# Attention block: the row maxima reach their contiguous row tile by tile, and the first score buffer gets its maximum behind its scores

## The reference

```python
x = x + attn(layernorm(x))      # softmax(q @ k.T * 64**-0.5) @ v for 16 heads, @ w_out + b_out
x = x + ffn(layernorm(x))       # fp4_linear(silu(fp4_linear(x, w_gate)) * fp4_linear(x, w_up), w_down)
```

## Time and profile before

| | us |
|---|---|
| median of 3 runs | 1384.71 |
| lowest, highest | 1379.86, 1384.8 |
| the profiled execution | 1384.4 |
| its span, first to last instruction | 1381.5 |
| TensorE busy | 1299.0 |
| GpSimd busy | 1053.9 |
| ScalarE busy | 897.7 |
| VectorE busy | 798.2 |

### The profile page before, as it was taken

How to read it: one execution, slowest core, us unless ns; L and a number is a source line. 1 busy time by engine, 2 the same in 40 slices (tenths; PEclk the granted TensorE clock), 3 DMA queues, 4 the chain that set the end, 5 groups by cost and what they waited for, 6 DMA issues and landing times.

```text
span 1381.5 us, 24376 instructions
## 1 busy us (share of the span) xinstructions
PE 1299.0 (94%) x7541; PEld 674.4 (49%) x7541; DVE 798.2 (58%) x2142; ACT 897.7 (65%) x1300; POOL 1053.9 (76%) x457
## 2 busy tenths in 40 slices
PE   4999999999999999999999999999999999898466
PEld 3555555555455555555445555555555454343245
DVE  6655555555455555555555555555555556777694
ACT  4767666677666766677666676667767667554242
POOL 4488878898778878888788888888988888789232
PEclk9999999999999999999999999999999999999787
DMA  2000000000000000000000000000000000000001
GB/s 61 2 9 2 1 2 9 2 1 1 3 9 2 2 1 9 2 1 1 3 9 2 2 1 9 2 2 1 3 1 1 1 2 1 2 1 1 1 1 30
DMA packets 18300, 6.63 MB, mean 5 GB/s; under 512 B 9696, under 2 KB 18016, under 8 KB 18160
## 3 DMA queue, kind: packets, MB, share of 16 engines
q1 hardware_dynamic: 17936, 4.40, 1.4%
q0 software_dynamic: 224, 0.54, 0.1%
HBM read 3.75 MB, written 1.05 MB: 3 GB/s over the span
## 4 chain that ended last, share of the span: by engine, by line
PE 85%; DVE 7%; issue 4%; POOL 2%; ACT 0%; DMA 0%; POOLq 0%; SPq 0%; DVEq 0%; ACTq 0%
PE o_ps L1151 32%; PE s_ps L1000 24%; PE mx_ps L1023 7%; PE mx_ps L1016 5%; PE misc_ps L1141 3%; PE s_ps L1008 2%; PE misc_ps L1133 2%; PE misc_ps L971 2%; PE misc_ps L983 1%; PE misc_ps L972 1%; PE misc_ps L973 1%; POOL acc_pool L497 1%; PE misc_ps L984 1%; PE misc_ps L985 1%; PE s_ps L1243 1%
## 5 line engine op out<-in xcount | busy, mean ns | idle before, releaser
L497 POOL TENSOR_TENSOR acc_pool<-acc_pool,probs 128x1024 f32<-128x1024 f32 x352 | 853.4, 2424 | 49.5 <-POOL acc_pool L497 40.3
L614 ACT ACTIVATE probs<-s_ps 128x1024 f32<-128x1024 f32 x512 | 527.3, 1030 | 122.1 <-PE s_ps L1008 67.3
L790 DVE CUSTOM_DVE_ANT_0 summed<-mx_ps,rise 128x512 bf16<-128x512 f32 x503 | 344.8, 686 | 424.9 <-issue 354.5
L1151 PE MATMUL o_ps<-probs,vv 128*64 128x512 f32 x2048 | 498.5, 607 | 5.1 <-ACT probs L614 5.1
L534 ACT ACTIVATE rise<-mx_ps 128x512 f32<-128x512 f32 x503 | 301.2, 599 | 271.7 <-PE mx_ps L1016 261.1
L1151 PEld LDWEIGHTS o_ps<-probs,vv 128*64 128x64 f32 x2048 | 127.2, 136 | 229.5 <-issue 174.8
L1016 PE MATMUL mx_ps<-k_raw,q_hi 64*128 64x512 f32 x503 | 224.5, 446 | 10.5 <-DVE part_max L790 9.2
L1023 PE MATMUL mx_ps<-k_hi,q_hi 64*128 64x512 f32 x503 | 224.5, 446 | 1.9 <-DVE part_max L790 1.8
L1000 PE MATMUL s_ps<-q_hi,k_hi 64*128 64x512 f32 x1024 | 207.0, 399 | 0.9 <-ACT probs L614 0.8
L1000 PE MATMUL s_ps<-q_hi,k_lo 64*128 64x512 f32 x1024 | 202.6, 390 | 0.0
L1000 PE MATMUL s_ps<-q_lo,k_hi 64*128 64x512 f32 x1024 | 202.4, 390 | 0.0
(11 more groups left out here) (161 smaller groups left out, 1119.0 us busy)
## 6 DMA issues: line engine op xcount, KB each, us to landing
wqkv<-in_L_attn_w_qkv SPq DMA_DIRECT2D x8, 192.0 KB, 3.3
y<-in_L_attn_x SPq DMA_DIRECT2D x4, 256.0 KB, 4.6
mrow<-neg_max SPq DMA_DIRECT2D x64, 2.0 KB, 2.0
out<-y SPq DMA_DIRECT2D x4, 256.0 KB, 2.3
wo<-in_L_attn_w_out SPq DMA_DIRECT2D x8, 64.0 KB, 1.9
wx<-in_L_ffn_w_down POOLq DMA_DIRECT2D x1, 176.0 KB, 6.6
wx<-in_L_ffn_w_gate POOLq DMA_DIRECT2D x1, 128.0 KB, 4.3
wx<-in_L_ffn_w_up POOLq DMA_DIRECT2D x1, 128.0 KB, 4.9
```

The lines of the kernel that those rows point to most:

```text
L497: pool.tensor_tensor(acc, first, probs[:, j % P_BUFS, :, :], ALU.add) \
L614: act.activation(probs[:, j % P_BUFS, :, :], s_ps[:, j % 2, :, :], ACT.Exp, scale=SCALE) \
L790: dve.tensor_tensor_reduce(summed[:, s % 2, :], mx_bank(h, pair), rise[:, h, :], 1.0, LOWEST, ALU.add, ALU.max, part_max[:, slot:slot + 1] ...
L1151: ins = pe.matmul(o_ps[DH * h:DH * (h + 1), :], vv[par(w)][:, j, DH * h:DH * (h + 1)], probs[:, j % P_BUFS, h, :], start=(j == 0), stop=(j ...
```

## The change

The reduction is made four times, once for each query tile `t`, as soon as that tile's last column is there (at `j` 6, 8, 10 and 12), and SP sends each tile's two columns with two DMAs of its own, 4 bytes from each partition, into 128 contiguous floats of `mrow`. So `mrow` is ordered tile first, and `maximum` reads it in order. `maximum(0)` of a unit is moved to the end of the unit before, directly behind the scores of its key block 0 at `j == 15`, ahead of the row-maximum step 15 and of two `weighted`; for the first unit it is in the prologue. TensorE's wait for `mrow_landed` moves with it.

```diff
-MAX_DONE = MAX_STEPS - AHEAD
-MAX_LAND = 32
+MAX_LAND = 128
+TILE_DONE = {MAX_STEPS - 2 * (TQ - 1 - t): t for t in range(TQ)}
-           + [("max", s) for s in range(4, MAX_STEPS + 1)] + [("neg", 0)]
-           + [("max", s) for s in range(MAX_STEPS + 1, MAX_STEPS + AHEAD)])
+           + [step for s in range(4, MAX_STEPS + AHEAD) for step in [("max", s)] + ([("neg", TILE_DONE[s])] if s in TILE_DONE else [])])
...
-            def max_row():
+            def max_row(t):
 
                 for h in range(2):
-                    sp.dma_start(mrow[DH * h:DH * h + 1, :].bitcast(F32).rearrange("o (q t) -> o q t", t=TQ),
-                                 neg_max[:, h * TQ:(h + 1) * TQ].bitcast(F32)).then_inc(mrow_landed, MAX_LAND // 2)
+                    n = h * TQ + t
+                    sp.dma_start(mrow[DH * h:DH * h + 1, t * P:(t + 1) * P].bitcast(F32),
+                                 neg_max[:, n:n + 1].bitcast(F32)).then_inc(mrow_landed, MAX_LAND // (2 * TQ))
...
-                        sp.wait_ge(negmax_ready, at(it, 1, w, 2))
-                        max_row()
+                        for t in range(TQ):
+                            sp.wait_ge(negmax_ready, at(it, TQ, w, TQ + t + 1))
+                            max_row(t)
...
-                dve.tensor_reduce(neg_max[:, :], part_max[:, :].rearrange("p (k n) -> p n k", k=GROUPS_MX),
+                dve.tensor_reduce(neg_max[:, :].rearrange("p (h t) -> p h t", t=TQ)[:, :, t],
+                                  part_max[:, :].rearrange("p (k h t) -> p h t k", k=GROUPS_MX, t=TQ)[:, :, t, :],
                                   AX.X, ALU.max, negate=True).then_inc(negmax_ready, 1)
...
-                        if j == MAX_DONE and runs(last, u, s):
-                            neg_maximum(max_no(it, w, j) + 1, at(it, 1, w, 2), at(it, MAX_LAND, w, MAX_LAND))
+                        done = TILE_DONE.get(j + AHEAD)
+                        if done is not None and runs(last, u, s):
+                            neg_maximum(done, max_no(it, w, j) + 1, at(it, TQ, w, TQ + done + 1),
+                                        at(it, MAX_LAND, w, MAX_LAND) if done == 0 else None)
...
-                    ins = pe.matmul(s_ps[:, buf, h, :].rearrange("p (t q) -> p t q", t=TQ), ones_r[rows, :],
-                                    mrow[rows, :].rearrange("p (q t) -> p t q", t=TQ), start=False, stop=True,
+                    ins = pe.matmul(s_ps[:, buf, h, :], ones_r[rows, :], mrow[rows, :], start=False, stop=True,
                                     skip_group_check=True)
...
             scores(0, 0, 0, 0)
+            pe.wait_ge(mrow_landed, MAX_LAND)
+            maximum(0).then_inc(s_ready, 1)
...
                     for j in range(STEPS):
-                        if j == 0:
-
-                            pe.wait_ge(mrow_landed, at(it, MAX_LAND, w, MAX_LAND))
-                            maximum(0).then_inc(s_ready, 1)
                         if j % 2 == 0:
                             row_maxima(it, w, last, j)
...
                             scores(0, par(w + 1), (w + 1) % Q_BUFS, 0)
+                            pe.wait_ge(mrow_landed, at(it, MAX_LAND, w, 2 * MAX_LAND))
+                            maximum(0).then_inc(s_ready, 1)
```

More of the change, by code:

```diff
@@ L380, in _ @@
             sp.dma_start(wqkv[:, :, :], wqkv_rows[:, :, 1, :]).then_inc(wqkv_loaded, 16)
-            def max_row():
+            def max_row(t):
                 for h in range(2):
-                    sp.dma_start(mrow[DH * h:DH * h + 1, :].bitcast(F32).rearrange("o (q t) -> o q t", t=TQ),
-                                 neg_max[:, h * TQ:(h + 1) * TQ].bitcast(F32)).then_inc(mrow_landed, MAX_LAND // 2)
+                    n = h * TQ + t
+                    sp.dma_start(mrow[DH * h:DH * h + 1, t * P:(t + 1) * P].bitcast(F32),
+                                 neg_max[:, n:n + 1].bitcast(F32)).then_inc(mrow_landed, MAX_LAND // (2 * TQ))
             sp.wait_ge(zeros_ready, ZEROED)
-            sp.wait_ge(negmax_ready, 1)
-            max_row()
+            for t in range(TQ):
+                sp.wait_ge(negmax_ready, t + 1)
+                max_row(t)
             def body(it, last):
@@ L791, in max_slot, with neg_maximum @@
                                          part_max[:, slot:slot + 1]).then_inc(mx_free, 1)
-            def neg_maximum(count, no, landed=None):
+            def neg_maximum(t, count, no, landed=None):
                 dve.wait_ge(mx_free, count)
@@ L863, in _ @@
                 else:
-                    neg_maximum(MAX_STEPS + 1, 1)
+                    neg_maximum(n, MAX_STEPS - 2 * (TQ - 1 - n) + 1, n + 1)
             split_weights(1, 2)
```

## The result

The changed kernel takes 1360.54 us (median of 6 runs, 1358.27 to 1364.91). Beside it the kernel before took 1381.3 us (6 runs). The ratio is 0.9845, with a 95% interval of 0.9828 to 0.9862: 1.55% faster, 20.8 us by the medians.

A forecast was written before the change was run, and what follows sets the result against it. TensorE's own stream was taken as the bound: 28 boundaries x 0.81 = 22.7 us, first unit -0.2, last three +0.6, total 23.1 off 1384.4, so about 1361.5 us as a median. Own range 1357 to 1366, widened to 1374 for rivals.

The forecast's parts named there:

- What bounds the kernel: From 60 to 1110 us TensorE waits for nobody but 5.4 us of issue; only shortening its own stream saves time.
- The sum of a boundary: At each unit boundary, 3.32 us before becomes 2.51 after: 0.81 us gained.
- Its two halves: The 0.81 us a boundary split into 0.41 by reading the row in order and 0.40 by removing the wait.
- Rival B: At the unit head the wait only changes its name; order alone counts, 11.5 us, time 1373; chance 0.08.
- What is late next: Output copy, then `rise` 0 ending near 702.9; TensorE asks at 703.5 (row-maximum step 1), leaving 0.6 us.
- Rival A: The step isn't what makes the L1008 maxima dear; only the wait goes, 11.2 us, time 1373; chance 0.09.
- Rival C: VectorE's extra reductions come through on TensorE: 0.9 us a unit eats 0.81, about 1385 to 1387; chance 0.07.
- The price of a reduction: Each new small VectorE reduction takes 0.3 us, bounds 0.2 and 0.4; three more make 0.9 us a unit, hidden.
- Rival D: Small transfers served one after the other, 2.0 us each, delay seven units waiting for `wo`: 57 us, time 1418; chance 0.04.
- point of decision: For serial transfers in units that wait for `wo`: it decides from 4.4 us of landing after the last issue.
- The first and the last units: First unit -0.2 us; last three gain 0.2, 1.0 and 0, less 0.6 for extra reductions; net +0.6.

The follow-up runs named there:

- order alone: The changed kernel with `maximum(0)` back at the head of the unit: 1377.16 us against 1382.49, ratio 0.996.
- place alone: The kernel before with the first maximum moved behind its scores; row, reduction and DMAs as they were: 1376.83 us, ratio 0.996.
- plain read: The kernel before with `mrow` read in order, so that the maxima reach other queries; sends and reduction unchanged: 1375.93 us, ratio 0.9954.
- sends alone: The kernel before with four reductions and eight DMAs, each tile to every fourth float: 1384.04 us against 1382.49, ratio 1.0007.
- late sends: The changed kernel with all eight DMAs sent behind the last tile: 1400.46 us with four reductions, 1408.33 us with one, against 1383.29.

## Why the prediction was right

It was right, in sign, mechanism and size: 1361.5 us forecast, 1360.54 measured, 23.1 us forecast on the profiled execution and 23.9 measured on the spans. Some of the closeness is luck. By the medians of six runs the change brings 20.8 us, and the forecast started from a median of three (1384.71) that lay 3.4 us above the 1381.3 of the six; the two differences largely cancel in the time. In the span of the profiles, 1.2 us come from the two returns of the loop, beyond what ordinary boundaries give, and for the greater part from a clock that fell in one execution and not in the other.

- **What bounds the kernel.** Right. TensorE waits for no other engine from 60 to 1080 us in either kernel, so its own stream is the time.
- **The sum of a boundary.** 0.81 forecast, 0.79 in the period and 0.80 at the boundary. The model "same work in mid-unit plus two quick pairs" carried it: it takes the whole from a stretch without the waits, not each wait by itself.
- **Its two halves.** 0.41 for order and 0.40 for the wait were right as parts of the sum, wrong as what each is worth alone: 0.21 and 0.30. Rival B priced order alone at 11.5 us, measured were 5.3. It overlooked that quicker pairs in front of scores 2 and `rise` 0 turn into longer waits for exponential 0 and for `rise` 0. It also read the price of the step from the second pair's 0.44 us, which in that kernel was a wait for exponential 0 as well; that the value was right is shown only by place alone (0.45 without a wait).
- **What is late next.** Copy and `rise` 0, 0.6 us of slack forecast, 0.67 measured.
- **Rival A.** Excluded by the plain read. The two rules weighed in the prediction can now be held against rows. The Trainium skill, "Advanced Engine Details and Errata", section "SBUF Cachelines", says that two hits on a 16-byte line are needed to hide the latency. Pairs of floats make two hits a line and still pay in full; only runs of four were quick. The free stride of 4 fp32 in the Trainium skill, "SBUF — State Buffer", section "Door 1: The DMA port swizzle", doesn't hold for the moving operand: a step of two pays already.
- **Rival C.** Excluded twice over, by sends alone and by 16 more reductions (1.45 us of VectorE a unit). The price of a reduction was mis-sized: 0.3 us with an upper bound of 0.4, but at step 8 it holds VectorE for 0.42, from the end of the sum's write at 669.27 to the normalisation:

```profile
669.31 0.16 DVE L800 TENSOR_REDUCE neg_max<-part_max 128x2 fp32r<-128x4 f32 x1
...
669.69 1.23 DVE L817 TENSOR_TENSOR o_norm<-o_raw,rden 128x512 f32<-128x512 f32 x1 [0.22 <-DVE neg_max L800]
```

  It cost nothing. I had counted a shift of the normalisation that fits into 1.13 us. In fact its end didn't move at all against POOL: before, L814 ends 0.54 us behind the end of a POOL addition (685.27 and 684.73), after, L817 too (670.92 and 670.38). Its duration fell from 1.87 to 1.23 us, as it started later and was held for less. VectorE's busy time rose by 9.7 us, less than the 15.2 that the reductions take more, as the normalisations are held for 11.6 less. With the waits behind its own reductions (39.6 us after, 15.0 before) it is some 34 in all, where 28 were forecast.
- **Rival D.** Excluded at this size; the landing is 2.0 us for each, overlapped. But its point of decision was nearer than I had it. An issue costs 0.62 us in a row of eight, not 0.56, and single ones take up to 1.33; the margin in the seven units with a `wo` load is 1.04 to 2.1 us, where the forecast had 2.4, and 1.0 at the worst landing. The late sends show the price on the other side of that margin: 40 us.
- **The first and the last units.** Unit 0 was forecast at -0.2 and gained 0.1. The last three were forecast at +0.6 and gained 0.6, but this is luck: unit 29 gained the 0.2 forecast, unit 30 2.2 instead of 1.0, and unit 31 lost 1.8, where 0 and the -0.6 for the reductions stood. Two terms are off by 1.2 us each and cancel. Which wait moved them was not tried apart.

## What to carry to other kernels

Price a boundary by the same work where it runs undisturbed, and take the difference; the parts of such a difference are not what each edit brings alone, since the edit that is missing leaves its bound standing. When a consumer is moved earlier, look at the last producer's queue, issue by issue: here sending the tiles early was worth nothing by itself, and with all eight sent late the move would have cost 40 us more. Where a matmul's moving operand is read with a step, look at runs of 16 bytes: here they were the shortest that were quick.

## What the runs showed of the hardware

- **A strided moving operand.** For 64x512 fp32r pairs at the upper clock (granted 1.00, 2.4 GHz): inside the stream 0.23 us to the next start in order (the changed kernel) and 0.45 at a step of four floats (place alone). As the opening pair of a unit 0.50 to 0.53 at a step of 2, 4 or 8 floats and in pairs of floats, and 0.34 in order and in runs of four.
- **A VectorE operation is held by GpSimd inside its own duration.** L827 took 2.67 instead of 0.55 us when it began 0.12 us behind a POOL addition, with no wait shown. The POOL addition behind it took 2.51 instead of 2.38. In the kernels before and after the split begins first, up to 0.07 us ahead of a POOL addition: it takes 0.55 us, and that addition 2.73 and 2.79. The Trainium skill, "SBUF — State Buffer", section "Who interferes with whom", says that a VectorE instruction with two inputs in SBUF contends with a GpSimd instruction that reads SBUF; the trace agrees, and adds that VectorE's busy time holds such standing still: L814 and L817 have 1.83 and 1.48 us a piece for the same work.
- **Small DMAs.** 256 of 128 elements with 4 bytes land like 64 of 128 elements with 16 bytes, median 2.0 us. What they cost is issue: 0.56 us in twos, 0.62 in eights, with single issues of up to 1.76 us in rows of eight (late sends with four reductions).
